# Two pairs of part buffers for the first features, residual stores awaited where their buffers are written again, attention maxima moved between groups

## The reference, cut to what matters

```python
xn = layernorm(x)                                    # x: 1250 nodes x 768
# 1. graph branch: three attention convolutions on the same x1, 4 heads each
x1 = relu(xn @ W_ah + b_ah)
for W, a_s, a_d, b in three layers:
    h = (x1 @ W).reshape(1250, 4, 192)
    e = leaky_relu(as_n[src] + ad_n[dst], 0.2)       # per edge and head
    m = segment_max(e, dst);  p = exp(e - m[dst])
    out = segment_sum(p * h[src], dst) / segment_sum(p, dst) + b
node_emb = relu of the three, side by side;  gnn = relu(node_emb @ W_out + b_out)
# 2. linear attention, 12 heads of 64
q, k = elu(q) + 1, elu(k) + 1                        # q, k, v = xn @ W_qkv.T
kv = k.T @ v;  mix = (q @ kv) / (q @ k_sum + 1e-6);  mix = mix @ W_proj.T + b_proj
x = x + gnn + mix
# 3. a small expert network on layernorm(x), added to x
```

## Time and profile before

| | |
|---|---|
| median of 3 runs | 1560.1 us (1557.59 to 1562.83) |
| the profiled execution's own time | 1562.15 us |
| its span, first to last instruction | 1560.1 us |
| mean granted clock of TensorE | 0.949 of full |
| PE busy, share of the span | 1420.6 us, 91% |
| DVE busy | 1066.4 us, 68% |
| ACT busy | 469.7 us, 30% |
| POOL busy | 36.5 us, 2% |

### The profile page before, as it was taken

The page is one execution under the profiler, slowest core; times in us unless marked ns, Lnnn a source line. Parts: engine busy times, 40 slices in busy tenths (PEclk is TensorE's granted clock), DMA queues, the critical chain, the costliest instruction groups (busy, mean ns, idle before and its releaser), DMA issues.

```text
span 1560.1 us, 21113 instructions
## 1 busy us (share of the span) xinstructions
PE 1420.6 (91%) x8180; PEld 1313.1 (84%) x8180; DVE 1066.4 (68%) x1950; ACT 469.7 (30%) x782; POOL 36.5 (2%) x41
## 2 busy tenths in 40 slices
PE   5998998999999687787999999999999999997788
PEld 4955666988888687687999999999999999997754
DVE  6858987888888632157667677667757766775654
ACT  3210123333333410133433343343243334222140
POOL 2100000000000021000000000000000000000000
PEclk9999999999999898788999999999999999999995
DMA  8310000122120374500110120111012011013003
GB/s 238 121 61 2 0 1 25 57 81 81 64 81 34 107 215 146 133 31 33 34 36 1 63 68 2 64 34 36 1 63 69 1 64 34 6 48 99 1 0 99
DMA packets 23300, 90.99 MB, mean 58 GB/s; under 512 B 3549, under 2 KB 4800, under 8 KB 20269
## 3 DMA queue, kind: packets, MB, share of 16 engines
q1 hardware_dynamic: 22289, 87.47, 17.7%
q10 hardware_dynamic: 924, 2.30, 0.5%
HBM read 78.70 MB, written 11.06 MB: 58 GB/s over the span
## 4 chain that ended last, share of the span: by engine, by line
PE 50%; DVE 8%; ACT 3%; issue 1%; DVEq 0%
PE psum L1494 21%; PE psum L101 8%; PE psum L102 8%; PE psum L103 8%; DVE prob L1222 2%; PE psum L1577 2%; DVE prob L1216 2%; DVE hN L1236 1%; ACT prob L1370 1%; PE psum L1508 1%; DVE x1l L1242 1%; PE psum L1545 1%; PE psum L1557 0%; ACT x1h L1376 0%; DVE acc L1257 0%
## 5 line engine op out<-in xcount | busy, mean ns | idle before, releaser
L1494 PE MATMUL psum<-hN,prob 125*125 125x193 f32 x2400 | 412.4, 328 | 10.8 <-DVE hN L1236 7.6
L1494 PEld LDWEIGHTS psum<-hN,prob 125*125 125x125 f32 x2400 | 397.6, 188 | 12.4 <-issue 9.3
L1370 ACT ACTIVATE prob<-prob,acol 125x1250 f32<-125x1250 f32 x120 | 160.9, 1341 | 396.6 <-DVE prob L1216 396.6
L1222 DVE SCALAR_TENSOR_TENSOR prob<-prob,cnt 125x1250 f32<-125x1250 f32 x120 | 174.8, 1456 | 80.2 <-ACT prob L1370 80.2
L1216 DVE SCALAR_TENSOR_TENSOR prob<-vrow,ncol,urow 125x1250 f32<-125x1250 f32 x120 | 181.9, 1515 | 0.0
L703 DVE CUSTOM_DVE_ANT_0 junk<-mask,arow 125x1250 bf16<-125x1250 uint8 x120 | 174.8, 1457 | 3.1
L101 PE MATMUL psum<-wph,x1h 128*125 128x384 f32 x360 | 135.1, 375 | 26.8 <-DVE x1l L1242 26.8
L101 PE MATMUL psum<-woh,xlh 128*125 128x384 f32 x360 | 129.0, 358 | 15.7 <-DVE acc L1257 15.7
L102 PE MATMUL psum<-wpl,x1h 128*125 128x384 f32 x360 | 128.2, 356 | 0.0
L103 PE MATMUL psum<-wph,x1l 128*125 128x384 f32 x360 | 128.2, 356 | 0.0
L102 PE MATMUL psum<-wol,xlh 128*125 128x384 f32 x360 | 124.5, 346 | 0.0
(11 more groups left out here) (202 smaller groups left out, 2197.2 us busy)
## 6 DMA issues: line engine op xcount, KB each, us to landing
arow<-scratch_a SPq DMA_DIRECT2D x12, 625.0 KB, 4.1
urow<-scratch_uv SPq DMA_DIRECT2D x12, 625.0 KB, 4.1
vrow<-scratch_uv SPq DMA_DIRECT2D x12, 625.0 KB, 5.9
wq_raw<-in_w_qkv SPq DMA_DIRECT2D x6, 1152.0 KB, 6.9
wp_raw<-in_w_pair SPq DMA_DIRECT2D x6, 1152.0 KB, 7.7
wo_raw<-in_w_out SPq DMA_DIRECT2D x6, 1152.0 KB, 5.8
wl<-in_w_gat SPq DMA_DIRECT2D x4, 1152.0 KB, 7.1
xN<-in_x SPq DMA_DIRECT2D x10, 336.0 KB
```

Of the source, the lines that this page charges most:

```text
L1222: nc.vector.scalar_tensor_tensor(prob[n % RING][:, :], prob[n % RING][:, :], 1.0, cnt[:, n % NT, :], op0=ALU.min, op1=ALU.mult).then_inc(p ...
L1370: nc.scalar.activation(prob[n % RING][:, :], prob[n % RING][:, :], ACT.Exp, bias=acol[:, n // NT, n % NT:n % NT + 1]).then_inc(e_ready, 1)
L1494: last = nc.tensor.matmul(bank(t // 2)[0:P, 193 * (t % 2):193 * (t % 2) + 193], ring[:, t * P:(t + 1) * P], hN[i % 2][:, j, 193 * s:193 * ...
```

## The change

Three edits, and what goes with them.

1. In `convolutions`, the tiles t = 1, 3, 5, 7, 9 of head pair 0 use a second pair of part buffers, x1h_odd and x1l_odd, which lie in the space of hN[1]. `x1_high(0, t)` no longer waits for `hidden(0, t-1)` but, from t = 2, for `hidden(0, t-2)`. GpSimd fills the columns of ones of hN[1] only after the tenth `hidden`; TensorE waits for those of hN[0] at period 0 and for those of hN[1] at period 1.
2. The wait of SP for the residual stores moves from the end of `projection` to three places in `convolutions`: SP ahead of its first row loads, VectorE ahead of the first `scores`, GpSimd ahead of its writes to hN[1].
3. In `attention` the 20 maxima of a period stand as 1, 1, 2, 4, 4 ahead of the five `k_features`, 2, 2, 2 ahead of the three `q_features`, and 2 at the end. Before it was 2, 2, 2, 2, 2, then 2, 2, 2, and 4.

```diff
@@ build
+        res_out = [ctx.enter_context(nc.semaphore(f"res_out{i}")) for i in range(4)]
@@ attention, vector
                 for gr in range(KG):
-                    maxima(2)
+                    maxima((1, 1, 2, 4, 4)[gr])
                     k_features(i, gr)
...
                     low_part(i + 1, slice(0, 128), q_high, q_low)
-                    maxima(4)
+                    maxima(2)
                 else:
                     for j in range(NG):
                         reciprocals(i, j)
-                    maxima(4)
+                    maxima(2)
@@ projection, sync
             sp.wait_ge(uv_out, 16)
             sp.wait_ge(wp_in, 16)
-            for i in range(4):
-                sp.wait_ge(res_out[i], 32 * len(range(i, NT, 4)))
@@ convolutions
+        x1h_odd = at("x1h_odd", S + 15456, [128, KT, P], F32R)
+        x1l_odd = at("x1l_odd", S + 15456 + 3008, [128, KT, P], F32R)
...
+        def x1_parts(i, t):
+            return (x1h_odd, x1l_odd) if i == 0 and t % 2 else (x1h, x1l)
@@ sync
+            for i in range(4):
+                sp.wait_ge(g["res_out"][i], 32 * len(range(i, NT, 4)))
             rows(0)
@@ gpsimd
+            nc.gpsimd.memset(eps[:, :], EPS).then_inc(eps_ready, 1)
             for i in range(2):
+                if i:
+                    pool.wait_ge(h_full, NT)
+                    pool.wait_ge(g["res_out"][0], 32 * len(range(0, NT, 4)))
                 nc.gpsimd.memset(hN[i][:, :, 0:1], 1.0).then_inc(ones_col, 1)
                 nc.gpsimd.memset(hN[i][:, :, PC + 1:PC + 2], 1.0).then_inc(ones_col, 1)
-            nc.gpsimd.memset(eps[:, :], EPS).then_inc(eps_ready, 1)
@@ vector
                 dve.wait_ge(xh_ready, NT * i + t + 1)
-                nc.vector.tensor_tensor(x1l[:, :, :], x1T[:, :, t * P:(t + 1) * P], x1h[:, :, :].bitcast(F32), ALU.subtract)\
+                high, low = x1_parts(i, t)
+                nc.vector.tensor_tensor(low[:, :, :], x1T[:, :, t * P:(t + 1) * P], high[:, :, :].bitcast(F32), ALU.subtract)\
                     .then_inc(xl_ready, 1)
...
+            def residual_stored():
+                for i in range(4):
+                    dve.wait_ge(g["res_out"][i], 32 * len(range(i, NT, 4)))
...
+                    if tile + AHEAD == 0:
+                        residual_stored()
                     if 0 <= tile + AHEAD - 1 < ALL:
                         weigh(tile + AHEAD - 1)
@@ scalar
             def x1_high(i, t):
-                if NT * i + t:
+                if i:
                     act.wait_ge(h_full, NT * i + t)
-                nc.scalar.activation(x1h[:, :, :], x1T[:, :, t * P:(t + 1) * P], ACT.Copy).then_inc(xh_ready, 1)
+                elif t >= 2:
+                    act.wait_ge(h_full, t - 1)
+                nc.scalar.activation(x1_parts(i, t)[0][:, :, :], x1T[:, :, t * P:(t + 1) * P], ACT.Copy).then_inc(xh_ready, 1)
@@ tensor
+                high, low = x1_parts(i, t)
                 for k in range(KT):
-                    last = split_matmul(nc, bank(5 + t % 3)[0:P, 0:PC], (x1h[:, k, :], x1l[:, k, :]),
+                    last = split_matmul(nc, bank(5 + t % 3)[0:P, 0:PC], (high[:, k, :], low[:, k, :]),
...
-            pe.wait_ge(ones_col, 4)
             for i in PERIODS:
+                if i in (0, 1):
+                    pe.wait_ge(ones_col, 2 * (i + 1))
```

More of the change, by code:

```diff
@@ L939, in projection @@
         x_in = [sem(f"xt_in{i}") for i in range(4)]
-        res_out = [sem(f"res_out{i}") for i in range(4)]
+        res_out = g["res_out"]
         low_in, wp_in, own_s = (sem(s) for s in "low_in wp_in own_s".split())
```

## The result

The changed kernel takes 1500.63 us (median of 4 runs, 1500.08 to 1501.98) against 1559.96 before (4 runs, 1557.59 to 1562.83). The ratio is 0.962, with a 95% interval of 0.9603 to 0.9638: faster by 59.3 us, where the forecast was 56.2 off the profiled execution and a median of 1504. The profiled execution of the changed kernel took 1500.28 us, its span is 1498.5.

The account below looks back on a forecast made before the run. Bounds: TensorE's waits for late reciprocals in attention, the store wait after projection, pauses in convolutions' period -1. Gains 25.9 + 2.1 + 28.2 = 56.2 us off 1562.15 give 1506.0, median 1504; range 1500 to 1509, 8 in 10 within 1497 to 1518.

Parts of the forecast that it names:

- Attention, four whole periods: Attention from the first turn: 170.91 us falls to 149 to 151, 21 saved, with VectorE setting the pace.
- The first wait: Attention period 1: TensorE's wait for yrow stays at 1.9 us because VectorE idles 3 us more in period 0; 2.1 saved.
- The end of attention: Last attention stretch: 3.3 us less maxima tail, 2.4 less low clock, some 3 lost to VectorE's lateness; net 2.8.
- Clock behind short waits: Attention: TensorE falls to no low clock after waits of 0.3 to 0.6 us; otherwise attention gains 24.4, not 25.9.
- Residual stores: End of projection: the gap to the next block falls from 2.59 to 0.5 us, gain 2.1, moved waits costing nothing.
- Two pairs of buffers: Convolutions, period -1: hidden tiles 3.18 us apart, pauses of 1.1 and 2.0 at the last two, scores 2 28.2 us earlier.
- (a): Attention: VectorE and ScalarE get in each other's way, late reciprocals; gain 15 rather than 25.9, 1515 us; chance 0.14.
- (b): Period -1 of convolutions: rows land late or clock sags; gain 18 to 23, 1509 to 1514 us; chance 0.12.
- (d): Attention: late reciprocals hold up the next period's keys, periods over 48 us; slower than before, 1564 us; chance 0.02.
- (e): Attention and convolutions: edits don't do what they say, only the store gap's 2.1 us stays; 1558 us; chance 0.02.
- rival (c): Whole kernel: VectorE has less to do than counted, or the low clocks vanish too; 1500 us; chance 0.08.
- The three terms: Gains summed: attention 25.9, store gap after projection 2.1, second buffers in convolutions' period -1 28.2; together 56.2 us.

Follow-up runs that it names:

- b1_more: The changed kernel with one of the maxima done twice at the end of attention periods 0 to 4; 1508.01 us, ratio 0.9661.
- b2_less: The changed kernel with the last two maxima of attention periods 0 to 4 taken over only a quarter of the nodes; 1497.44 us, ratio 0.9585.
- e4_split: The kernel before with maxima 2, 2, 2, 3, 3 ahead of the k features, 2, 2, 2 ahead of the q features, 2 at the end; 1531.69 us.
- d1_spread: The changed kernel with 24 maxima in attention period 0, 19 in each of periods 1 to 4, 20 in period 5; 1498.72 us, ratio 0.9598.
- d2_all: The changed kernel with early prob tiles, head 0's normalise two links earlier and maxima spread 24, 19, 19, 19, 19, 20; 1497.6 us, ratio 0.9614.
- c2_normalise: The changed kernel with four prob tiles made during the hidden tiles and head 0's normalise two chain links earlier; 1496.29 us, ratio 0.9601.
- e2_buffers: The kernel before with the second pair of part buffers alone, SP's store wait left at the end of projection; 1530.41 us, ratio 0.9797.
- after_again: The changed kernel measured once more, with nothing altered, beside the later runs; 1498.44 us, ratio 0.9597.
- e1_maxima: The kernel before with the new split of the attention maxima alone; 1532.39 us, ratio 0.9808.

## Why the prediction was right

**Attention, four whole periods.** Forecast 149 to 151 us, measured 149.19. The reason holds by `b1_more` and `b2_less`: VectorE 37.3, TensorE 37.1. One step was off: I forecast waits of 0.3 to 0.6 us in each later turn, because I let VectorE's order cost more than its sum. None was recorded. That the order can cost something beyond the sum is true of `e4_split`, 0.7 us a period, not of this order.

**The first wait.** Forecast 1.9, measured 1.54. The cause given, that VectorE waits longer in period 0, is borne out with a smaller size: 6.7 us against 4.9 before, so 1.8 more and not 3. The cure that `d1_spread` tried was not one. The saving was put down as 2.1, though 3.74 less 1.9 is 1.84. The wait fell by 2.2, but the stretch from the first keys to the first turn only from 52.77 to 51.53, by 1.2: the rest was lost ahead of the wait. Other traces of the old order have 53.8 for this stretch, others of the new one 50.4 to 51.7.

**The end of attention** was mis-sized: from the last turn to the next block 38.82 us before, 34.73 after, 4.1 gained where I had 2.8 (my terms add up to 2.7). The two gains were right: 3.2 from the shorter tail of maxima, for which I had 3.3, and 2.3 from the slow work behind the last wait, for which I had 2.4. The loss was too high: from the fourth turn to ScalarE's last copy it took 14.7 us before and 16.2 after, so VectorE's lateness costs 1.5 and not 3. Of this, 0.8 is the longer wait for the last q feature, 2.57 against 1.76.

In all attention gained 27.1 in these two traces, forecast 25.9. Against the other traces of the old order (264.74 and 264.85) it is some 29; a part of that lies ahead of the first wait and a part in the clock behind each wait, which I had as 1.4 to 2.5 us from the one trace I had and which reached 2.8.

**Clock behind short waits.** I took none behind waits under 1 us. The changed kernel did not test this, as it had no such waits; `e4_split` did. There waits of 0.72 us came every 38 us, the next turn followed after 5.31 us against 6.6 to 7.7 behind the long waits, and the granted clock was 1.00. The rule of the Trainium skill (TensorE: Matmul & The Clock Gate, A second HAM failure mode), by which small frequent pauses would cost clock, did not apply to pauses of this size and distance. Longer ones fell on both sides: behind turn waits of 1.54 us and, in `d2_all`, of 1.77 the next turn came after 5.31 too, behind the 1.88 of `d1_spread` after 6.90. These few rows give no limit.

**Residual stores.** 2.07 against 2.1. The row loads were issued late as forecast and no scores waited for them.

**Two pairs of buffers.** 27.8 against 28.2; the cadence 3.15 against 3.18; the pauses 1.22 and 1.73 against 1.1 and 2.0. The low term is hidden 0, 5.68 us from its start to the next where I had 5.3. The chain from scores 2 to the restart kept its 46.7 us in both traces. That it sets the restart agrees with `c2_normalise`, where moving normalise two links forward brought the restart 5.4 us earlier.

**The rivals.** (a) did not come about: four maxima ahead of the last kf held nothing up that counts, and no wait of TensorE for a bank stands in these periods. (b) did not: from 600.00 to 618.30 the granted clock was 1.00 at a DMA share of 0.78, and no scores waited for rows. (d) and (e) fell: a period takes 37.3 us and not 48, and the restart moved by 27.8. The median, 1500.6, lies at the 1500 of rival (c), but not for its reason that VectorE has less to do: VectorE was busy 36.37 us a period with 0.9 us of gaps, 37.3 in all. The three terms measured 56.9 where the forecast had 56.2, and would give 1503. The other 2.4 us of the 59.3 between the medians, or 4.7 between the traces, lie in stages that nobody touched, and no edit accounts for them. That the time came out inside the range is due to the three terms; how far below 1504 it lies is mostly chance.

## What to carry to other kernels

Work that nothing waits for soon is best put behind the instruction that someone does wait for, up to the point at which the two engines have equal sums. After that point less work on one of them brings little, here 0.2 us of the 2.0 a period; it would take less on both. And a busy share of 100% does not name the engine that sets the pace: TensorE was shown busy for the whole period, yet the 1.51 us added to VectorE came through in full. A second buffer pays by what it lets start earlier further down the chain, so find the instruction that sets the restart and count to it. And when a wait is removed inside an engine's serial chain, look at the next tile before believing the gain: with `c2_normalise` the restart came 5.4 us earlier and the rest took 6.4 longer.

## What the hardware showed that I had not expected

The pauses of one length did not cost one price. Behind waits of 3.73 to 3.74 us the next turn came 6.6 to 8.1 us later, against 5.3 behind no wait, by how long the matmuls ran at the lower of the two clock levels. With five such waits attention took 262.5 us in one trace and 264.7 to 264.9 in two others; in `e2_buffers` 1.3 of the 2.2 us came from this and 1.0 from ahead of the first wait. Whether a program with such pauses also varies more from run to run is not shown: before ranged over 1557.59 to 1562.83 us and the changed kernel over 1500.08 to 1501.98, but over 1496.86 to 1501.06 in `after_again`, and `e1_maxima`, without the five long waits, over 1526.4 to 1535.15.

Two engines could be nearly full at the same time, TensorE 37.30 us busy of 37.30, of which `b2_less` shows 37.1 to be its own work, and VectorE 36.37 with 0.9 us of gaps between its instructions, while handing results to each other several times a period.
